# Attention scores turned before the exponential, and attended values divided on another engine

## The reference

```python
q, k, v = layernorm(x) @ wq + bq, ctx @ wk + bk, ctx @ wv + bv       # 16 heads of 16
score = einsum('bhqd,bhkd->bhqk', q, k) / sqrt(16) * mask
score = where(score == 0, -1e9, score)
context = einsum('bhqk,bhkd->bhqd', softmax(score), v)
x = x + tanh(g_xattn) * (context @ wo + bo)
logits = layernorm(x) @ router_w + router_b                          # 4 experts, top 2
gates = softmax over the two largest of softmax(logits)
h = silu(xn @ w1[e]) * (xn @ w3[e])
x = x + tanh(g_ffn) * sum_e gates[e] * (h @ w2[e])
```

## Time and profile before

| | |
|---|---|
| median of 3 runs | 511.23 us |
| lowest, highest | 510.8, 513.08 us |
| span of the profiled execution, first to last instruction | 514.2 us (no other time of it is given) |
| busy in it | PE 485.6, DVE 400.4, ACT 316.7, POOL 188.1 us |
| mean granted clock of TensorE | 0.971 |

### The profile page before, as it was taken

One profiled execution on the slowest core, in us unless ns is written; L12 is line 12 of the kernel. 1 busy time (PEld: TensorE's weight loads), 2 busy tenths in 40 slices (PEclk: granted clock), 3 DMA queues, 4 the chain that ended last, 5 costly groups with the idle time before them and its releaser, 6 DMA issues.

```text
span 514.2 us, 11413 instructions
## 1 busy us (share of the span) xinstructions
PE 485.6 (94%) x3622; PEld 443.5 (86%) x3622; DVE 400.4 (78%) x940; ACT 316.7 (62%) x759; POOL 188.1 (37%) x191
## 2 busy tenths in 40 slices
PE   9889999999888999999999999999999999999991
PEld 7557777777666899999999999999999999999880
DVE  2687898898997588888688888888878788887550
ACT  3224457556433766587577676677767777777760
POOL 2524656448765305263035263112202220222111
PEclk9996999999987999999999999999999999999996
DMA  8999885000211311323112232022212111211110
GB/s 269 355 388 395 358 314 206 21 22 12 74 43 48 119 31 38 62 43 60 26 18 43 70 65 42 23 42 31 33 24 42 21 30 22 31 22 23 20 12 10
DMA packets 32392, 45.13 MB, mean 88 GB/s; under 512 B 9709, under 2 KB 28781, under 8 KB 32109
## 3 DMA queue, kind: packets, MB, share of 16 engines
q1 hardware_dynamic: 24807, 34.66, 19.9%
q0 software_dynamic: 6576, 8.92, 10.5%
q10 hardware_dynamic: 960, 0.94, 0.6%
HBM read 33.50 MB, written 21.82 MB: 108 GB/s over the span
## 4 chain that ended last, share of the span: by engine, by line
PE 68%; DVE 17%; issue 5%; POOL 4%; ACT 3%; ACTq 1%; DVEq 0%; POOLq 0%
PE ps_scores L1782 21%; PE ps_wide L1802 7%; PE ps_probT L1782 7%; PE ps_misc L1802 7%; PE ps_wide L1607 5%; DVE w_lo L1413 3%; PE ps_misc L1629 3%; PE ps_scores L1578 2%; PE ps_scores L1831 2%; DVE w_lo L1409 2%; PE ps_misc L1552 1%; POOL score L1100 1%; DVE lowest L1267 1%; PE ps_probT L1588 1%; PE ps_wide L1842 1%
## 5 line engine op out<-in xcount | busy, mean ns | idle before, releaser
L1176 POOL DMA_INDIRECT out_x<-y_out,meta x35 | 63.6, 1817 | 194.5 <-ACT y_out L974 189.4
L1413 DVE TENSOR_TENSOR w_lo<-w,w_hi 128x512 fp32r<-128x512 f32 x152 | 104.3, 686 | 16.1 <-ACT w_hi L931 8.3
L1782 PE MATMUL ps_scores<-xt_hi,w_hi 128*128 128x256 f32 x384 | 110.9, 289 | 0.2 <-DVE xt_lo L1427 0.2
L1782 PE MATMUL ps_scores<-xt_lo,w_hi 128*128 128x256 f32 x384 | 108.8, 283 | 0.0
L1782 PE MATMUL ps_scores<-xt_hi,w_lo 128*128 128x256 f32 x384 | 108.8, 283 | 0.0
L931 ACT CAST w_hi<-w 128x512 fp32r x152 | 95.5, 629 | 4.7 <-issue 4.3
L1782 PEld LDWEIGHTS ps_scores<-xt_hi,w_hi 128*128 128x128 f32 x384 | 73.7, 192 | 0.4 <-DVE xt_lo L1427 0.4
L1782 PEld LDWEIGHTS ps_scores<-xt_lo,w_hi 128*128 128x128 f32 x384 | 73.8, 192 | 0.0
L1782 PEld LDWEIGHTS ps_scores<-xt_hi,w_lo 128*128 128x128 f32 x384 | 73.7, 192 | 0.0
L945 ACT ACTIVATE act_g<-ps_scores 128x256 f32<-128x256 f32 (+1 forms) x114 | 42.3, 371 | 36.7 <-PE ps_scores L1782 23.2
L1100 POOL TENSOR_TENSOR score<-score,lowest 128x616 f32<-128x616 f32 x32 | 38.9, 1215 | 52.5 <-DVE lowest L1267 52.1
(11 more groups left out here) (237 smaller groups left out, 1233.1 us busy)
## 6 DMA issues: line engine op xcount, KB each, us to landing
grouped<-in_pad SPq DMA_DIRECT2D x1, 10296.0 KB
w<-in_L_ffn_w SPq DMA_DIRECT2D x8, 1024.0 KB, 12.5
w2s<-in_L_ffn_w SPq DMA_DIRECT2D x4, 1024.0 KB, 13.6
xg<-grouped SPq DMA_DIRECT2D x16, 256.0 KB, 2.7
out_x<-xall SPq DMA_DIRECT2D x8, 256.0 KB
xall<-in_x SPq DMA_DIRECT2D x1, 1024.0 KB, 13.1
xall<-in_x SPq DMA_DIRECT2D x1, 768.0 KB, 7.3
ctxT<-in_ctx_t SPq DMA_DIRECT2D x2, 308.0 KB, 5.0
```

The lines of the kernel that those rows point to most:

```text
L1176: pool.indirect_dma_start(out, bass.IndirectOffsetOnAxis(ap=meta[:, s % 2, t, E:E + 1].bitcast(U32), axis=0), y_out[:, s % 2, t, :], None, ...
L1413: dve.tensor_tensor(w_lo[:, f % NB], unit_weights(e, f), w_hi[:, f % NB].bitcast(F32), ALU.subtract).then_inc(w_lo_done, 1)
L1782: mm = pe.matmul(ps_gu[f % NB][:, m, 0:n], lhs, rhs[:, a, c, 0:n], start=(k == 0), stop=(k % (3 * DC) == 3 * DC - 1), skip_group_check=True)
```

## The change

The scores are transposed as they come from `lower`; ACT takes the exponential where it copied, from PSUM into `probT`. `prob` and its exponent pass are gone. After attend, ACT copies the 128x136 values of the step, the sums of the heads among them, from PSUM into a new SBUF tile, `weighed`, and attend waits for that copy. DVE takes the reciprocals of two steps at once from SBUF (`invert_sums`), and POOL multiplies (`context`, 128x256 elements for two steps); the very last such product is DVE's. `turn_ctx` moves behind the scores of the next batch.

```diff
-        prob = sb("prob", [P, 2, HG * SK], stack=att)
+        weighed = sb("weighed", [P, 2, NS, HG, VH])
+        rden = sb("rden", [P, DC, QT, HG])
...
+        def context(eng, b, g):
+            eng.wait_ge(rden_done, DC * b + g + 1)
+            if b > 1:
+                eng.wait_ge(ctxT_done, b - 1)
+            eng.tensor_tensor(ctxn[:, b % 2, :, g * HG:(g + 1) * HG, :], weighed[:, b % 2, QT * g:QT * (g + 1), :, 0:DH],
+                              rden[:, g].unsqueeze(3).to_broadcast([P, QT, HG, DH]), ALU.mult).then_inc(ctx_done, 1)
...
ACT
-                    act.copy(probT[:, s % 2, 0:4], ps_probT[:].rearrange("p (c n) -> p c n", c=4)).then_inc(turned_copied, 1)
+                    act.activation(probT[:, s % 2, 0:4], ps_probT[:].rearrange("p (c n) -> p c n", c=4), ACT.Exp, scale=-1.0 / UNIT).then_inc(turned_copied, 1)
                     act.wait_ge(turned, 2 * n + 2)
-                    act.copy(probT[0:ROWS[4], s % 2, 4], ps_probT4[0:ROWS[4], :]).then_inc(turned_copied, 1)
+                    act.activation(probT[0:ROWS[4], s % 2, 4], ps_probT4[0:ROWS[4], :], ACT.Exp, scale=-1.0 / UNIT).then_inc(turned_copied, 1)
+                def weighed_copy(b, s):
+                    act.wait_ge(av_done, NS * b + s + 1)
+                    if b > 1 and s % QT == 0:
+                        act.wait_ge(ctx_done, DC * (b - 2) + s // QT + 1)
+                    act.copy(weighed[:, b % 2, s], ps_av[:, s // QT]).then_inc(weighed_done, 1)
...
                     if not first:
-                        probT_copy(b - 1, 3, False)
+                        weighed_copy(b - 1, 2)
+                        probT_exp(b - 1, 3, False)
                     if not last:
                         xT_copy(b + 1)
...
                         norm2(act, BEGIN[b], range(0, 2))
+                        weighed_copy(b, 0)
+                        turned2_copy(act, BEGIN[b], 0)
+                        probT_exp(b, 1, first)
                         ctxT_copy(b - 1)
-                        turned2_copy(act, BEGIN[b], 0)
-                        probT_copy(b, 1, first)
-                        exponent(b, 2, first)
                         norm2(act, BEGIN[b], range(2, GN))
+                        weighed_copy(b, 1)
                         turned2_copy(act, BEGIN[b], 1)
-                        probT_copy(b, 2, first)
-                        exponent(b, 3, first)
+                        probT_exp(b, 2, first)
...
POOL
+                    if not first:
+                        context(pool, b - 1, 0)
                     lower(b, 0)
...
                         scatter(pool, FINAL[b - 1], COPIES[4:6])
+                    if not first:
+                        context(pool, b - 1, 1)
                     lower(b, 2)
...
                 body(B - 1, last=True)
+                context(pool, B - 1, 0)
...
DVE
-                        dve.wait_ge(exp_done, n + 1 - NS)
+                        dve.wait_ge(turned, 2 * (n + 1 - NS))
...
+                def invert_sums(b, g):
+                    dve.wait_ge(weighed_done, NS * b + QT * (g + 1))
+                    if b:
+                        dve.wait_ge(ctx_done, DC * (b - 1) + g + 1)
+                    dve.reciprocal(rden[:, g], weighed[:, b % 2, QT * g:QT * (g + 1), :, DH]).then_inc(rden_done, 1)
...
                         sink_zeros(b, s)
-                        if ends:
-                            pass
-                        elif s == NS - 1:
-                            finish(b, 0, False)
-                        elif not (s == 1 and routing):
-                            finish(b - 1, s + 1, False)
+                        if s % QT == 0:
+                            invert_sums(b - 1, s // QT)
                         find_lowest(b, s)
...
PE
-                    pe.wait_ge(exp_done, n + 1)
+                    pe.wait_ge(lowered, n + 1)
...
-                        mm = pe.transpose(ps_probT[:, c * P:(c + 1) * P], prob[:, s % 2, c * P:(c + 1) * P], ident)
+                        mm = pe.transpose(ps_probT[:, c * P:(c + 1) * P], score[:, s].rearrange("p h k -> p (h k)")[:, c * P:(c + 1) * P], ident)
...
-                        pe.wait_ge(ctx_done, n)
+                        pe.wait_ge(weighed_done, n)
...
                     attend(b, 0, first)
-                    if not first:
-                        turn_ctx(b - 1, last)
                     turn_p(b, 1, first)
...
                     if not last:
                         scores(b + 1, 0, False)
+                    if not first:
+                        turn_ctx(b - 1, last)
                     attend(b, 1, first)
```

More of the change, by code:

```diff
@@ L832, in q_copy, with probT_exp @@
                     act.activation(qT[:, 1, :], ps_misc[:, SQ:], ACT.Identity, bias=bqs[:, 1:2]).then_inc(q_copied, 1)
[L834 to L842, removed]
+                def probT_exp(b, s, first):
                     n = NS * b + s
@@ L862, in body @@
                     if not first:
-                        probT_copy(b - 1, 3, False)
+                        weighed_copy(b - 1, 2)
+                        probT_exp(b - 1, 3, False)
                     if not last:
                         xT_copy(b + 1)
[L866 to L871, removed]
+                    if not first:
+                        weighed_copy(b - 1, 3)
+                    probT_exp(b, 0, first)
                     if last:
@@ L1267, in find_lowest @@
                     dve.tensor_reduce(lowest[:, s], score[:, s], AX.X, ALU.min).then_inc(lowest_found, 1)
-                def divide(b, s, first):
-                    n = NS * b + s
-                    dve.wait_ge(av_done, n + 1)
-                    if not (first and s == 0):
-                        dve.wait_ge(ctx_done, n)
-                    dve.reciprocal(rden[:], ps_av[:, s // QT, :, DH]).then_inc(rden_done, 1)
-                def context(b, s):
-                    n = NS * b + s
-                    g, t = s // QT, s % QT
-                    dve.wait_ge(rden_done, n + 1)
-                    if b > 1:
-                        dve.wait_ge(ctxT_done, b - 1)
-                    dve.tensor_tensor(ctxn[:, b % 2, t, g * HG:(g + 1) * HG, :], ps_av[:, g, :, 0:DH],
-                                      rden[:].unsqueeze(2).to_broadcast([P, HG, DH]), ALU.mult).then_inc(ctx_done, 1)
-                def finish(b, s, first):
-                    divide(b, s, first)
-                    context(b, s)
+                def invert_sums(b, g):
[3 more added lines that the diff above has]
+                    dve.reciprocal(rden[:, g], weighed[:, b % 2, QT * g:QT * (g + 1), :, DH]).then_inc(rden_done, 1)
                 def values(c, i):
@@ L1311, in body @@
                                 off_mean(2)
[L1312 removed]
                         if s == 0 and b in FINAL:
                             invert(dve, FINAL[b])
[L1315 to L1329 removed]
+                        if s == 1 and b in BEGIN:
+                            variance2(dve, BEGIN[b])
+                        sink_zeros(b, s)
+                        if s % QT == 0:
+                            invert_sums(b - 1, s // QT)
                         find_lowest(b, s)
@@ L1397, in _ @@
                     body(b)
-                finish(B - 1, 1, False)
+                invert_sums(B - 1, 0)
                 hand_out(dve, 1)
@@ L1401, in _ @@
                 residual(B - 2)
-                finish(B - 1, 2, False)
                 hand_out_owner(dve, 1)
                 hand_out_rest(dve, 1)
-                finish(B - 1, 3, False)
+                invert_sums(B - 1, 1)
+                context(dve, B - 1, 1)
                 def w2_lo_of(s, e, q):
@@ L1595, in turn_p_end @@
                         pe.wait_ge(turned_copied, 2 * n)
-                    pe.transpose(ps_probT4[0:ROWS[4], :], prob[:, s % 2, 4 * P:4 * P + ROWS[4]], ident).then_inc(turned, 1)
+                    pe.transpose(ps_probT4[0:ROWS[4], :], score[:, s].rearrange("p h k -> p (h k)")[:, 4 * P:4 * P + ROWS[4]], ident).then_inc(turned, 1)
                 def attend(b, s, first):
```

38 lines of the change are left out of this document (14 added, 24 removed).

## The result

The changed kernel takes 510.38 us (median of 20 runs, 506.7 to 511.68) against 513.14 us (20 runs, 510.8 to 516.77) for the kernel before, run beside it: ratio 0.9939, 95% interval 0.992 to 0.9958. The forecast was 503.3 us, and the time lies 0.9 us above the upper end of the range. The kernel before spreads over 6 us from one execution to the next, the one after over 5, with 17 of its 20 between 509.6 and 511.7 us. And an execution's own time is its span plus a nearly fixed amount, 1.8 us for the kernel after and 1.9 to 2.1 us for the kernel before: the profiled one after took 510.4 us with a span of 508.6 us.

The account below looks back on a forecast made before the run. PE bounds it, DVE from 126 to 146 us. 2.1 (waits) + 2.9 (DVE) - 0.2 (exponential) - 0.3 (end) + 5.1 (low clock) - 1.7 (low expert start) = 7.9 us off: 503.3 us, range 498.5 to 509.5 us.

Parts of the forecast that it names:

- the first low stretch: Attention stage, 36 to 56 us: granted clock 0.74 and 0.75 behind a PE lull, priced at 5.1 us lost.
- 2.1 + 5.1: PE waits of 1.52 and 0.64 us removed, 2.1 us in sum, plus 5.1 us of early low clock recovered.
- DVE's relief: Between 123 and 163 us, eight step pairs: 3.9 us off DVE, 1.0 us of reciprocals on, net 2.9 us.
- a loss of 0.2: Exponential out of PSUM on ScalarE: 0.02 us later on eight steps without cover, 0.2 us, at most 1.1.
- The end of the stage: Last context product stands behind seven GpSimd scatters; PE waits 2 to 5 us at last turn_ctx; 0.3 us given back.
- the three prices: Low clock behind three PE lulls, from 36, 136 and 156 us: 5.1, 1.7 and 3.4 us lost.
- The first low stretch did not stay: Rival, chance 0.20: low clock after 36 us stays, as two PE pauses before the first attend remain; 508.4 us.
- the second rival: Chance 0.12: GpSimd's products land on DVE's two-input score pass or push the subtraction into it, 9.9 us; about 513 us.
- the fourth rival: Chance 0.08: GpSimd becomes the bound, products near 1.53 us, low clock behind the last wait; 515.7 us, up to 517.
- All waits recovered: Rival, chance 0.13: last subtraction early enough that GpSimd is through in time, clock stays up; 12.3 us off, 499 us.
- 0.3 + 1.7 us: Last turn_ctx behind GpSimd's scatters: 0.3 us given back, plus 1.7 us for a low-clock start of the expert stage.
- The rule that the prediction quoted: GpSimd shares SBUF interfaces with VectorE and contends with two-SBUF-input instructions; up to a product's length lost per meeting.

Follow-up runs that it names:

- the rank experiment: Kernel with the last product but one on DVE, plus the routing's rank products moved behind project_o in batches 4 and 6: 509.86 us, ratio 0.9941.

## Why the prediction was wrong

**The span was missed by 2.3 us, the time by 7.1.** The forecast span was 506.3 us, the measured one 508.6 us. The other 4.8 us lie in one step, the one that failed most: "The profiled execution spans 514.2 us, 3.0 us over the median of the timed runs (511.23); 506.3 us of span is then 503.3 us in their terms". A span must get 1.8 us added to become a time, and 3.0 us were subtracted: the step compared the span of one execution with the times of others. The profiled execution's own time, about 516 us with the 1.9 us of the kernel before, was among the slowest of the kernel before, whose runs go from 510.1 to 516.8 us. With that step done right the same sum gives 508.1 us and misses by 2.3. (The forecast's own range was also set a little wide of its terms: they give 501.6 to 505.9 us, and 501 to 506.5 us were stated.)

**The low stretch was taken for a fixture.** "5.1 us more if the first low stretch goes" is a gain against the profiled execution alone. The change did remove it, together with the waits: batch 2's turning of xn starts at 58.13 us. In the kernel before it starts at

```profile
64.90 0.66 PE L1545 MATMUL ps_misc<-small,xn 128*128 128x128 f32 x4
...
131.92 0.66 PE L1545 MATMUL ps_misc<-small,xn 128*128 128x128 f32 x4 [0.34 <-ACT xn L813]
```

so 6.8 us against the forecast 7.2 (2.1 + 5.1). But the second profile of the kernel before, without any low stretch there, is at 62.43 us: against it 4.3 us are won, 3.7 of them its four waits up to there (1.52, 0.24, 1.07 and 0.84 us). That also says the low stretch cost 2.5 us in the end and not 5.1 (2.9 us counted from the second attend, which came 0.44 us later in the second profile). At the full clock PE waited more: 0.24 and 1.07 us at places where the slow PE had no wait, and 0.84 where it had 0.64 us. Adding one minus the clock over a stretch overstated the loss here, where another engine set the pace.

**DVE's relief: 2.9 forecast, 2.0 found.** From batch 6's turning of xn to the last subtraction the profiles read 162.65 - 131.92 = 30.73 us before and 153.27 - 124.51 = 28.76 us after. Waits for logits (1.00 us) and chosen_b (1.22 us) are still there; the second grew from 0.6 us, as PE had won more on its way there than DVE. The last subtraction came 9.4 us earlier than in the earlier trace rows (9.9 by the sum): 6.8 and 2.0 us as above, and 0.6 us between the two places, where the sum had a loss of 0.2.

**The end of the stage: mechanism right, one size wrong.** The GpSimd chain was foreseen: turn_ctx 9.6 us behind the last subtraction, measured 9.5; a wait of 2 to 5 us, measured 3.82; turn_ctx 9.6 us earlier than before, measured 9.2. The term that was mis-sized is "I charge 1.7 us, the smallest of the three prices". From turn_ctx to the first expert matmul were 3.82 us before and are 7.38 us now: 3.56 us, about the middle one of the prices listed (3.4 us), and the kernels with matmuls in the wait confirm some 3 us. The 0.4 us by which the last turn_ctx fell short and the 1.9 us by which 3.56 exceeds 1.7 are the whole miss of the span. The expert stage is 337.2 us in both. The wait was to stand there once; in the second profile of the change it is split in two, 1.86 us at batch 6 and 2.77 us at the end.

**Where the gain of a typical execution went.** Against the second profile of the kernel before: the last subtraction is 6.9 us earlier (160.21 against 153.27 us), the last turn_ctx 4.0 us, the first expert matmul 0.4 us. 3.0 us were given back to the scatters, 3.6 to the clock. What is left of the measured 2.8 us in the median is, it seems, that the kernel before has low stretches in many of its executions and the changed one has lost the first. This last split rests on two profiles and the clocks of the runs; how often each stretch comes was not counted.

**The rivals.** The first low stretch did not stay. GpSimd's time did not land on the wide passes of DVE (959 ns) and its product was not dear (0.62 us), so neither the second rival nor the fourth is what happened, though the fourth rival's last link, a product behind the scatters with a low clock after it, took most of the gain. All waits recovered (499 us) was too much for every kernel here; the lowest median is 504.5 us. The prediction treated the place behind the scatters as fixed and priced it at 0.3 + 1.7 us. It was worth 5.7 us side by side, and one moved product gets it back.

## What to carry to other kernels

Before a sum is made against a profile, ask whether that execution is a typical one: compare its own time (span plus the constant that the runs show) with the runs' spread, and count no low stretch as a gain unless a second profile has it. When work is moved to another engine, look at the last instance first: there a queue of DMA issues that nobody waits for can stand ahead of the one product that everybody waits for. A short wait on PE costs what it says plus the low clock that may follow; filling it with idle matmuls separates the two prices.

## What was not expected of the hardware

The same kernel, with the same waits to a hundredth of a microsecond, runs the stretch behind a 1.5 to 1.7 us wait at a granted clock of 0.71 to 0.75 in one execution (means over ten microseconds) and at 1.00 in another. The changed kernel does the same behind its 1.22 us wait for chosen_b: 0.66 from 139 to 143 us in one profile, 1.00 in the other. Behind the last wait of the changed kernel (3.82 us in one profile, 2.77 us in the other) it was low both times, down to the lower level, 1.2 GHz, as the 3.51 us of the route product against 2.00 us show.

Small two-input instructions of DVE that start beside a tensor operation of GpSimd last until about its end. The product of 128x256 takes DVE 0.42 us alone and 1.33 us where it starts beside GpSimd's subtraction (152.92 to 154.14 us), in the second profile of the kernel with the product on DVE:

```profile
153.09 1.33 DVE L316 TENSOR_TENSOR ctxn<-weighed,rden 128x256 f32<-128x256 f32 x1
...
159.94 0.42 DVE L316 TENSOR_TENSOR ctxn<-weighed,rden 128x256 f32<-128x256 f32 x1
```

The 128x32 and 128x4 instructions shown for the rank experiment (1.82 and 1.83 us; others of these shapes take 0.16 to 0.19 us) do the same behind a product and a subtraction in a row. Between 36 us and the end of the stage twelve or thirteen small instructions of DVE are stretched to 0.56 to 1.5 us; counted against 0.18 us (0.26 us for the 128x64 ones) that is 10.0 us in the kernel before and 11.4 us after, so the new product adds little to it. The rule that the prediction quoted from the Trainium skill (GPSIMD Engine Reference, Key points) thus holds here. It shows on the wide pass that reads `score` twice (up to 1.62 us before and 1.40 us after, against 0.77 us at the shortest), as the rival said, but no more after the change than before it; and it shows on small instructions, which nobody had priced.
